# Four fused graph layers on one NeuronCore: first and last pass reordered (squares ahead of weight work, two first heads scored without stacking, values one chunk later)

## What is computed

```python
x = _layernorm(x + _L0_gnn_ref(x, adj, Wq, Wk, Wv))      # rel = adj.T * (q k^T); rel / norm(rel, axis=2); rel @ v
x = _layernorm(x + _L1_gnn_ref(x, adj, weight, bias))    # D^-1/2 adj D^-1/2 (x W) + bias
x = _layernorm(x + _L2_gnn_ref(x, adj, adj, ...))        # 3 gated steps (GRU-like), each with adj @ h
x = _layernorm(x + _L3_gnn_ref(x, adj, ...))             # 8-head attention, head size 32, masked by adj
```

## Time and profile before

| | us |
|---|---|
| median of 3 runs | 2070.99 (2067.48 to 2071.02) |
| the profiled execution | 2068.63 |
| its span in the trace | 2066.8 |
| TensorE busy (share of the span) | 1997.2 (97%) |
| DVE, ScalarE, POOL busy | 1542.1 (75%), 1277.5 (62%), 1034.8 (50%) |
| first 120 us, 12 windows of 10: TensorE busy 2.14 to 10.00 of 10 | lowest from 30 to 40 |
| 1990 to 2060, 7 windows of 10 | TensorE busy 7.13 to 8.22 of 10 |

### The profile page before, as it was taken

How to read it: one execution, slowest core, us unless ns; L and a number is a source line. 1 busy time by engine, 2 the same in 40 slices (tenths; PEclk the granted TensorE clock), 3 DMA queues, 4 the chain that set the end, 5 groups by cost and what they waited for, 6 DMA issues and landing times.

```text
span 2066.8 us, 34564 instructions
## 1 busy us (share of the span) xinstructions
PE 1997.2 (97%) x12214; PEld 1633.0 (79%) x12214; DVE 1542.1 (75%) x3442; ACT 1277.5 (62%) x2629; POOL 1034.8 (50%) x1153
## 2 busy tenths in 40 slices
PE   6889999999999999999999999999999999999986
PEld 4667888887888788888887888888888887888764
DVE  5567777777777878777777777878777777877756
ACT  3335757576575766757576575756657576675745
POOL 2224545546364554645456464554645555454546
PEclk8999999999999999999999999999999999999999
DMA  4003022130211203112130212213012130302222
GB/s 138 1 21 72 11 62 52 41 72 21 54 40 43 72 21 72 42 42 52 41 72 21 66 27 57 57 32 72 31 42 52 42 72 21 72 22 61 52 52 62
DMA packets 65631, 101.14 MB, mean 49 GB/s; under 512 B 11440, under 2 KB 31152, under 8 KB 65456
## 3 DMA queue, kind: packets, MB, share of 16 engines
q1 hardware_dynamic: 65456, 98.87, 18.9%
HBM read 23.34 MB, written 8.39 MB: 15 GB/s over the span
## 4 chain that ended last, share of the span: by engine, by line
PE 91%; DVE 3%; ACT 3%; issue 1%; POOL 1%; SPq 0%; DMA 0%; DVEq 0%; POOLq 0%; ACTq 0%
PE ps L1054 18%; PE ps L1056 17%; PE ps L1055 17%; PE ps L1076 12%; PE ps L1173 10%; PE ps L1193 6%; PE ps L1157 5%; PE ps L1482 2%; ACT fa L563 1%; PE ps L1253 1%; DVE xn L782 1%; PE ps L1389 1%; PE ps L1286 1%; ACT pT L446 1%; PE ps L1333 0%
## 5 line engine op out<-in xcount | busy, mean ns | idle before, releaser
L336 POOL TENSOR_SCALAR fa<-fa,rsum 128x512 f32<-128x512 f32 x512 | 454.9, 900 | 54.5 <-POOL rsum L330 54.5
L330 POOL TENSOR_TENSOR rsum<-esum,mhalf 128x2 f32<-128x2 f32 x256 | 198.6, 776 | 533.3 <-ACT fa L451 531.5
L808 DVE CUSTOM_DVE_ANT_0 fa<-ps,mask 128x512 f32<-128x512 f32 x512 | 332.1, 686 | 134.9 <-PE ps L1157 129.8
L451 ACT ACTIVATE fa<-fa,nmax 128x512 f32<-128x512 f32 x512 | 367.6, 728 | 18.9 <-DVE nmax L808 18.9
L446 ACT COPY pT<-ps 128x512 f32<-128x512 f32 x480 | 277.1, 584 | 130.3 <-PE ps L1173 129.4
L1173 PE MATMUL ps<-ident,fa 128*128 128x128 f32 x1920 | 287.3, 275 | 7.9 <-ACT pT L446 5.7
L1173 PEld LDWEIGHTS ps<-ident,fa 128*128 128x128 f32 x1920 | 228.7, 140 | 80.6 <-issue 23.8
L795 DVE TENSOR_TENSOR ra<-ps,ra 128x512 fp32r<-128x512 f32 x224 | 151.1, 687 | 164.5 <-ACT ra L601 89.0
L1076 PE MATMUL ps<-adjT,ra 128*128 128x512 f32 x1024 | 252.4, 397 | 3.2 <-DVE ra L947 3.2
L1076 PEld LDWEIGHTS ps<-adjT,ra 128*128 128x128 f32 x1024 | 192.4, 191 | 46.0 <-issue 3.5
L325 POOL TENSOR_TENSOR rstd<-veps,mhalf 128x2 f32<-128x2 f32 x128 | 98.2, 773 | 167.6 <-DVE veps L758 143.1
(11 more groups left out here) (203 smaller groups left out, 4706.6 us busy)
## 6 DMA issues: line engine op xcount, KB each, us to landing
ra<-ra SPq DMA_DIRECT2D x512, 128.0 KB, 2.3
fa<-in_x_T SPq DMA_DIRECT2D x17, 512.0 KB, 4.7
fa<-in_x SPq DMA_DIRECT2D x17, 512.0 KB, 3.9
out<-fa SPq DMA_DIRECT2D x15, 512.0 KB, 3.0
fa<-in_L_gnn_w_w SPq DMA_DIRECT2D x3, 512.0 KB, 10.5
adj_n<-in_adj SPq DMA_DIRECT2D x1, 1024.0 KB, 8.6
fa<-in_L_gnn_u_w SPq DMA_DIRECT2D x2, 256.0 KB, 9.7
out<-xn SPq DMA_DIRECT2D x2, 256.0 KB, 2.1
```

The source lines that it names most:

```text
L330: nc.gpsimd.tensor_tensor(rsum[:, 2 * k:2 * k + 2], esum[:, 2 * k:2 * k + 2], mhalf[:, 4:6], ALU.pow).then_inc(rs_r, 1)
L336: nc.gpsimd.tensor_scalar(SC[:, g], SC[:, g], rsum[:, 2 * k + u:2 * k + u + 1], 1.0, ALU.mult, ALU.mult).then_inc(nrm, 1)
L451: nc.scalar.activation(SC[:, s % RING], SC[:, s % RING], ACT.Exp, bias=nmax[:, s:s + 1], scale=-1.0, accum_out=esum[:, s:s + 1]).then_inc( ...
L808: nc.vector.tensor_tensor_reduce(out=SC[:, s % RING], in0=ps[:, (4 if i is not None else lone_bank(k)) + u], in1=mask[:, 2 * (k % 8 // 4) ...
```

## The change

First pass: POOL does `squares(0)` directly behind the split of x, then the low part of `W["w1"]`, the norm, and only then the power for the degrees. TensorE's four matmuls L1286 write bank 7 and no longer wait for `UB` (they wait for the adjacency, whose tile used that bank). Two of DVE's weight sums (L692, L693) move behind the copy of the sums of squares, and `flag_and_degrees` behind `sums_and_statistics`.

Last pass: the transposes of x3 stand ahead of `values(o, 3)`; the first two q/k products need the output parts (`ot_l`) no more, the second writes bank 1. Heads 0 and 1 of the first query half are scored straight from q and k (`direct_score`: for each tile three matmuls over 32 partitions), the others from the stack, whose transfers now begin with heads 2 and 3. v is made ahead of the q and k of the second head group, which move into the loop's surroundings. `values(t, m)` is issued one chunk later. DVE masks the first scores ahead of its addition for o (L892).

```diff
-            return 0 if alone and k == 3 else QK_BANK[k]
+            return 1 if alone and k == 1 else QK_BANK[k]
...
                     for n in range(HEADS):
                         gr, slot = n // 4, n % 4
-                        if slot == 0:
+                        if n < 4 and i is None:
+                            slot = (n + 2) % 4
+                        if n % 4 == 0:
                             sp.wait_ge(qk_l, t * 4 + (2 * gr + 2))
-                        if n == 2 and i is None:
+                        if n == 0 and i is None:
                             sp.wait_ge(a_ps, t * 6 + 6)
-                        elif n == 2:
+                        elif n == 2 and i is not None:
                             sp.wait_ge(qk_ps, t * 4 + 4)
...
+                    squares(i)
+                    if i == 0:
+                        gp.wait_ge(s_act, w1_h + 1)
+                        nc.gpsimd.tensor_tensor(W["w1"][:, L], st1, f32(W["w1"][:, H]), ALU.subtract).then_inc(s_pool, 1)
+                    gp.wait_ge(ssq_c, i + 1)
+                    nc.gpsimd.tensor_tensor(rnorm[:, :], ssq[:, :], mhalf[:, 0:NT], ALU.pow).then_inc(rn_r, 1)
                     if i == 0:
                         gp.wait_ge(s_dve, deg + 1)
                         nc.gpsimd.tensor_tensor(dtmp[:, 2, :], dtmp[:, 1, :], mhalf[:, 0:NT],
                                                 ALU.pow).then_inc(s_pool, 1)
-                        gp.wait_ge(s_act, w1_h + 1)
-                        nc.gpsimd.tensor_tensor(W["w1"][:, L], st1, f32(W["w1"][:, H]), ALU.subtract).then_inc(s_pool, 1)
-                    squares(i)
-                    gp.wait_ge(ssq_c, i + 1)
-                    nc.gpsimd.tensor_tensor(rnorm[:, :], ssq[:, :], mhalf[:, 0:NT], ALU.pow).then_inc(rn_r, 1)
                     rstd_of(0, i)
...
-                    qk_hi(2)
-                    qk_hi(3)
                     exponentials(t, 0)
                     exponentials(t, 1)
                     act.wait_ge(vv_ps, t + 1)
                     copy(vf[:, :, :], natural(6)).then_inc(vv_r, 1)
+                    qk_hi(2)
                     exponentials(t, 2)
...
+                        if k == 0:
+                            qk_hi(3)
                         if k + 3 < CHUNKS:
...
                 TT(st3[:, :, 0:D], st3[:, :, 0:D], st4[:, :, 0:D], ALU.subtract).then_inc(s_dve, 1)
+
+            def other_sums():
                 TT(st5[:, :, 0:D], st5[:, :, 0:D], st5[:, :, D:2 * D], ALU.add).then_inc(s_dve, 1)
                 TS(stu5, stu5, 0.5, None, ALU.mult).then_inc(s_dve, 1)
...
                     dve.wait_ge(ssq_ps, i + 1)
-                    nc.vector.tensor_copy(ssq[:, :], ps[:, 0, 0:NT]).then_inc(ssq_c, 1)
+                    nc.vector.tensor_copy(ssq[:, :], ps[:, SSQ_BANK if first else 0, 0:NT]).then_inc(ssq_c, 1)
+                if first:
+                    other_sums()
                 if t is not None:
...
                 if i is None:
+                    masked(0)
                     dve.wait_ge(yo_ps, o * 2 + 2)
                     dve.wait_ge(xc_r, o + 1)
                     TT(X4, natural(4), X4, ALU.add).then_inc(x4a, 1)
-                    masked(0)
+                    masked(1)
                     qk_lo(2)
-                    masked(1)
-                    qk_lo(3)
                     masked(2)
...
+                        if k == 0:
+                            qk_lo(3)
                         if k + 4 < CHUNKS:
...
                     dve.wait_ge(rn_r, i + 1)
                     if first:
-                        flag_and_degrees()
                         dve.wait_ge(s_pool, w1_l + 1)
                     sums_and_statistics(0, o_ps, rnorm, XIN)
                 if first:
+                    flag_and_degrees()
                     dve.wait_ge(s_pe, flag_ps + 1)
...
-                if o is not None:
+                if o is not None and i is not None:
...
                     adjacency(3)
                 if t is not None:
+                    if i is None:
+                        pe.wait_ge(pt_c, o * TILES + TILES - 2)
                     pe.wait_ge(x3_r, t + 1)
                     for d in range(DT):
                         for s in range(NT):
                             ins = nc.tensor.transpose(ps[:, 4 + d, s * P:(s + 1) * P], x3[:, s, d * P:(d + 1) * P],
                                                       ident[:, :])
                         ins.then_inc(x3_ps, 1)
+                if i is None:
+                    values(o, 3)
                 if i is not None:
                     pe.wait_ge(xs_l, i + 1)
                     for s in range(NT):
...
                     pe.wait_ge(x3_l, t * 2 + 2)
                     if isinstance(t, int) and t == 0:
                         pe.wait_ge(s_pool, wd_l + ND - 1)
-                    if o is not None:
+                    if o is not None and i is not None:
                         pe.wait_ge(ot_l, o * 2 + 2)
                     qk_of(0)
                 if i is not None:
-                    pe.wait_ge(u_l, i * 2 + 1)
+                    if first:
+                        pe.wait_ge(s_dve, adjT_l + NT)
+                    else:
+                        pe.wait_ge(u_l, i * 2 + 1)
                     pe.wait_ge(sq_s, i * 3 + 3)
                     for s in range(NT):
-                        ins = mm(ps[:, 0, s:s + 1], REL[:, 0, s * P:(s + 1) * P], ones1[:, :], start=True, stop=True)
+                        ins = mm(ps[:, SSQ_BANK if first else 0, s:s + 1], REL[:, 0, s * P:(s + 1) * P], ones1[:, :], start=True, stop=True)
                     ins.then_inc(ssq_ps, 1)
                 if t is not None:
                     qk_of(1)
+                def direct_score(k):
+                    pe.wait_ge(qk_l, t * 4 + 2)
+                    if k == 1:
+                        pe.wait_ge(x4a, o + 1)
+                    r = slice(k * HD, (k + 1) * HD)
+                    for u in range(2):
+                        dst, c = ps[:, lone_bank(k) + u, :], slice(u * P, (u + 1) * P)
+                        mm(dst, SRC[r, 1, H, c], SRC[r, 1, 2 + H], start=True, stop=False)
+                        mm(dst, SRC[r, 1, L, c], SRC[r, 1, 2 + H], start=False, stop=False)
+                        mm(dst, SRC[r, 1, H, c], SRC[r, 1, 2 + L], start=False, stop=True).then_inc(sc_ps, 1)
+
                 def lone_score(k):
+                    if k in (4, 5):
+                        pe.wait_ge(stk[k % 4], t * 128 + 64)
                     if k % 8 < 4:
                         pe.wait_ge(stk[k % 4], t * 128 + 64 * (k // 8 + 1))
-                    if k == 1:
-                        pe.wait_ge(x4a, o + 1)
                     for u in range(2):
-                        if k >= 2:
-                            pe.wait_ge(ttr, t * TILES + (2 * k - 3 + u))
+                        pe.wait_ge(ttr, t * TILES + (2 * k - 3 + u))
                         q = 2 * (k % 8 // 4) + u
                         rows = stacked(k % 4, True)
                         mm(ps[:, lone_bank(k) + u, :], rows[:, 0, q * P:(q + 1) * P], rows[:, 1, :],
...
                 if i is None:
                     pe.wait_ge(ot_l, o * 2 + 2)
                     natural_tiles(4, OT, W["wo"], 0, yo_ps)
+                    direct_score(0)
                     natural_tiles(4, OT, W["wo"], 1, yo_ps)
+                    natural_tiles(6, X3T, W["wv"], 0, None)
+                    direct_score(1)
+                    natural_tiles(6, X3T, W["wv"], 1, vv_ps)
                     qk_of(2)
-                    lone_score(0)
-                    qk_of(3)
-                    lone_score(1)
-                    pe.wait_ge(qk_l, t * 4 + 2)
-                    natural_tiles(6, X3T, W["wv"], 0, None)
                     lone_score(2)
-                    natural_tiles(6, X3T, W["wv"], 1, vv_ps)
                     lone_score(3)
...
+                        if k == 0:
+                            qk_of(3)
                         if k + 4 < CHUNKS:
                             lone_score(k + 4)
-                        if k % 4 == 3:
-                            values(t, k // 4)
+                        if k % 4 == 0 and k > 0:
+                            values(t, k // 4 - 1)
+                    values(t, 3)
```

More of the change, by code:

```diff
@@ L158, in gnn_stack @@
         wt_l, bv_r, biases = 9 + NT, 9 + NT + NW, 10 + NT + NW
-        consts, deg_r, w1_l, wq_s, wd_l, mask_r = 0, 5, 6, 7, 8, 7 + ND
+        consts, w1_l, deg_r, wq_s, wd_l, mask_r = 0, 5, 6, 7, 8, 7 + ND
+        SSQ_BANK = 7
         W3_LOADS = 4 + 1 + 8 + 2
@@ L1324, in body @@
                                 pe.wait_ge(vv_r, t + 1)
-                                pe.wait_ge(qk_l, t * 4 + 4)
                             elif c == 0:
```

## The result

The changed kernel takes 2055.22 us, median of 4 runs (2054.02 to 2056.67), against 2070.09 (2067.48 to 2071.02, 4 runs) before: a ratio of 0.9931, interval 0.9920 to 0.9943. It is 14.9 us faster. The prediction had 2056.3. The profiled executions differ by less: 2068.63 before, 2056.67 after, spans 2066.8 and 2054.8, so -12.0.

The account below looks back on a forecast made before the run. TensorE bounds passes 1 to 15, taken as unchanged; dependency chains bound the ends. First pass -4.4 and last -8.6 make -13.0, from 2068.63 to 2055.6, stated as 2056.3 us because the profiled execution lies below the median; range 2051.5 to 2061.5.

Parts of the forecast that it names:

- Step 1: First pass: POOL's three square additions, begun at 26.2, end near 30.2, where they ended at 37.88.
- Step 2: First pass: one DVE addition collides with POOL's w1 work, costing 1.1 (0 to 3.2); `UB` ready at 34.65.
- Step 3: First pass: layer 0's products begin at 34.75 instead of 39.72, DVE's sum 5.0 sooner; half clock kept, full clock 1.2 sooner.
- Step 4: First pass: flag work and its trip now stand between the statistics and L936, costing 0.6 (0.3 to 1.5).
- it is kept: First pass: the gain of 4.4 lasts, as everything to the pass's end hangs on this chain and all loads have landed.
- The q product: Last pass: x3 transposes fill TensorE's idle time, so the q product starts at 1994.25 instead of 1996.98, -2.7.
- the second rival: Clock rises sooner: last-pass values at full clock (-1.8), layer 0's products too (-1.2); -16.0, 2053.3 us; chance 0.08.
- Chunk 2's row sum: Last pass: TensorE's own list sets chunk 2; POOL's row sum comes at 2011.3 instead of 2017.50, -6.2.
- POOL never idles: Last pass, chunks 5 to 15: POOL needs 2.24 each and its idle times of 1.52 and 0.80 vanish, -2.3.
- The first rival: Last pass's loop gives nothing back, new POOL idle times as long as the old; -10.0, 2059.3 us; chance 0.19.
- The third: Last pass: chunks 2 to 5 still wait for stack or DVE despite direct scores; -6.5, 2062.8 us; chance 0.06.
- no change or slower: Last pass's loop: TensorE keeps half clock; all of it at half clock gives 2078 us; chances 0.03 and 0.02.

Follow-up runs that it names:

- e5: Changed kernel with POOL doing the norm's power before the low part of w1 in the first pass; 2054.01 us, ratio 0.9924 to the kernel before.
- e3: Changed kernel with the values in the last pass's loop issued in the chunk where they stood before; 2058.34 us, ratio 0.9949 to the kernel before.
- e4: Changed kernel with the last pass's x3 transposes put back behind the values of element 14; 2059.26 us, ratio 0.9951 to the kernel before.
- e7: Changed kernel with all heads scored from the stack in its old order, v ahead of second q and k; 2058.96 us.
- e8: Changed kernel with 14 matmuls nobody reads in TensorE's first-pass gap behind the column sums; 2053.11 us, ratio 0.9924 to the kernel before.
- e6: Changed kernel with flag_and_degrees put back ahead of the first layer's sums; 2054.48 us, ratio 0.9933 to the kernel before.
- e1: Kernel before with only the first pass's edits, last pass as before; 2063.26 us, ratio 0.9968 to the kernel before.
- e9: Changed kernel with the second head group's q and k moved behind chunks 0 and 1 in the last pass; 2053.85 us.
- e11: Changed kernel with 14 unread matmuls in the first pass and the second head group's q and k one step later; 2051.41 us.
- e10: Changed kernel with w1's low part behind the norms, nine unread matmuls, and the second head group's q and k one step later; 2053.43 us.

## Why the prediction came out as it did

The total was right: 2056.3 for 2055.22, and both mechanisms held (e5 for the collision, e3, e4 and e7 for the last pass). By its own steps:

First pass, -4.4. Step 1, squares from 26.2: measured 26.60, ending 30.53 for "near 30.2"; 0.3 of both is the later first square. Step 2, one collision of 1.1: shown (e5), `UB`'s low part at 33.66 for 33.4. By the rule of the Trainium skill ("SBUF — State Buffer", Who interferes with whom) the estimate was 1.2, and e5 is its direct test: 1.76 beside the w1 instruction, 0.68 without. Step 3, the wv product -5.0 at half clock: measured -5.0 after the first square, and half clock it was (0.66); e8 gives the 1.2 that was named as its price. Step 4, +0.6: `any_lo` stands 0.58 behind the last statistics, where it followed at once, so 0.5 on DVE, near the forecast. But it was added to the whole, and there it did not arrive: the way from the first sum to `any_lo` is only 0.2 longer than before, since the second sum no longer waits for TensorE (0.19 before), and the gather came the full 5.0 sooner (e6: no difference at the gather). What I had as "it is kept" was the larger miss: the -5.0 at the gather is -3.5 at the next element's input in this trace, behind orders that did not change and at another clock. Across the seven traces with the first pass of the changed kernel (in e6 but for the flag), that landmark lies between 102.52 and 105.11, before at 108.58 and 108.49. So the step is worth 3.4 to 6.1 there by execution, and e1's median says 6.0.

Last pass, -8.6: measured -9.3.
1. The q product -2.7: measured -4.4 (4.85 after tr14 for 9.22). Of the 1.7 beyond it 1.5 is the values' clock. I had read the 0.67 of 1990 to 2000 as the work of the idle time of 2.11; but the clock had fallen at about 1987.7, ahead of it, and was back at about 1994.4 before it began. This is the half of the second rival that came true; its other half, full clock in layer 0, did not.
2. All q and k at 0.24, -1.5: measured -1.6 (2.85 from the q product to the output product for 4.42).
3. Chunk 2's row sum -6.2, chunk 5's -5.6: measured -7.3 and -6.7. With the 1.5 of the clock taken out chunk 2 is -5.8, so the sum had 0.4 too much. The direct scores cost 0.23 each, over 32 partitions as over 128, the price that I took with no row for it. But on top of the -5.9 of items 1 and 2 they and the new order bring chunk 2 only 1.3 nearer, where I had 2.0. What stands in the way is named by e9: with the second group's q and its split moved from ahead of chunk 2 it comes 2.3 sooner, counted from the q product.
4. POOL never idles, -2.3: from chunk 5 to 15 it came 2.3 nearer. e3 prices the edit by itself at 3.1, since a third idle time of 0.68 appears without it.
5. The output product, -0.7: measured -0.3.

The first rival (the loop gives nothing back) is out by e3. The third (chunks 2 to 5 still wait for something that moved little) is out as TensorE names no transfer there. The last of them, no change or slower, needed half clock in the loop; 2030 to 2040 shows 1.00. The rule of the Trainium skill that would have favoured it ("TensorE: Matmul & The Clock Gate", Part 4: transposes do not count as busy) disagrees with the traces. The clearest is e9's, here in the transposes of x3 and in the values behind them:

```profile
1985.36:1987.10 1.74, 1.74 (x9) 1.51 (x8) 0.03 (x1) 1.17 (x2) 0.00 (x0) 0.50 0.04 9
1987.20:1989.07 1.87, 1.87 (x34) 0.94 (x33) 1.25 (x2) 0.59 (x1) 1.72 (x3) 1.00 0.00 0
```

When the clock rose, just ahead of the first of the values, nothing but twelve transposes had run on TensorE since 1984.45. Whether these matmuls with an identity use the mode that the page means, no trace tells.

That the total lies so near the median is in part luck. The traces moved by -12.0, less than the -13.0 of the sum; the medians by -14.9. The profiled execution of before lies 1.5 under its median, that of after is the highest of its four. The clock also took 1.5 of the first pass and gave 1.5 to the last, neither of which was in the sum.

## What to carry over

Time a two-ended change by stretches between landmarks, not by spans: start-up and clock moved single executions by 1 to 3 us here, as much as most of these edits are worth. In a place where the engine that bounds the end has just been idle, put whatever is ready first: the transposes of x3 filled an idle time, hid a split, and in ten of eleven traces took most of the lower clock in place of the values, 3.8 us for one moved line in e4's trace. And when an engine becomes the pacemaker of a loop (POOL, 2.24 a chunk), look for the one large item in another engine's list that stands between it and its inputs, and move that by one chunk (e9: 1.2 us from the q product to the end; the whole times do not tell it from the changed kernel).

## What the runs showed that I had not expected

- A gain of the first pass can be taken by the clock later. Pass 1 took 124.5 to 124.7 in twelve traces and 127.2 to 127.3 in two (e1, e11) with the same instructions; the clock over its first 20 us was 1.00 in the short ones read for it (before, after, e10) and 0.83 in the long ones. What decides between the two stays open: both long ones had gained in the gather, but so had e10, which did not lose it.
- Behind a wait of 1.40 all twelve q and k matmuls of e4 were 0.23 apart, while behind the 2.11 of the kernel before some took 0.43.
- Fourteen matmuls whose result nobody reads cost no time (the wv product at 9.57 for 9.55) and gave 1.2 us to the first sum; the next element's input still has them (103.88 for 105.11).
